# Erf of three batches as a tanh with a polynomial on GpSimd, and later statistics, in a four-layer cross-attention kernel

## What is computed

```python
# layer 2: 16 heads of 16
attn = softmax(Q @ K.T / sqrt(16));  ctx = attn @ V
out = q + gelu(ctx @ Wo + bo, approximate=False)      # x * (1 + erf(x / sqrt 2)) / 2, added to the row

# layer 3: 8 heads of 32
x = residual + mha(layernorm(x), layernorm(ctx))
xn = layernorm(x);  U = (xn @ W_in.T + b_in) @ Bmat
s = silu(s @ A.T) + u_t                                # 512 steps, one after the other
x = x + states @ Cmat + mean(probs) @ W_prog.T + b_prog
```

## Time and profile before

| what | value |
|---|---|
| median of 3 runs | 1514.4 us |
| the profiled execution, its own time | 1517.49 us |
| its span in the trace | 1515.9 us |
| PE, DVE, ACT, POOL busy | 1346.9, 1039.8, 1065.2, 82.9 us |
| mean granted clock of PE | 0.961 |
| scores of the first quad of turns 0 to 3 start at | 341.44, 586.93, 860.87, 1139.6 us |

### The profile page before, as it was taken

The page is one execution under the profiler, slowest core; times in us unless marked ns, Lnnn a source line. Parts: engine busy times, 40 slices in busy tenths (PEclk is TensorE's granted clock), DMA queues, the critical chain, the costliest instruction groups (busy, mean ns, idle before and its releaser), DMA issues.

```text
span 1515.9 us, 35932 instructions
## 1 busy us (share of the span) xinstructions
PE 1346.9 (89%) x13436; PEld 1002.6 (66%) x13436; DVE 1039.8 (69%) x2323; ACT 1065.2 (70%) x3212; POOL 82.9 (5%) x145
## 2 busy tenths in 40 slices
PE   7999899988998889999888999988899999788855
PEld 6788666665675556777666677766676777566644
DVE  4676757756787778687777777877776787777400
ACT  4556677757788887777787677777866777787422
POOL 2000111110000000000000000000000000000000
PEclk9999999999999999999999999999999999999855
DMA  8222310012221122121101211201121121110100
GB/s 296 85 87 98 103 56 2 1 46 95 58 85 42 44 75 68 42 71 57 57 30 57 83 31 58 85 29 54 47 70 43 43 85 57 29 50 9 43 0 14
DMA packets 69883, 90.42 MB, mean 60 GB/s; under 512 B 5520, under 2 KB 58896, under 8 KB 69328
## 3 DMA queue, kind: packets, MB, share of 16 engines
q1 hardware_dynamic: 69600, 87.87, 18.2%
q0 software_dynamic: 112, 0.26, 0.1%
HBM read 71.33 MB, written 16.78 MB: 58 GB/s over the span
## 4 chain that ended last, share of the span: by engine, by line
PE 60%; DVE 14%; ACT 14%; issue 10%; POOL 0%; DMA 0%; ACTq 0%; DVEq 0%; SPq 0%; POOLq 0%
PE ps L1320 14%; PE ps L1694 11%; PE ps L1327 8%; PE ps L1334 7%; PE ps L1723 6%; ACT arena L790 5%; DVE arena L1269 5%; PE ps L1768 3%; PE ps L1397 2%; PE ps L1521 2%; PE ps L1538 2%; PE ps L1677 2%; DVE arena L949 2%; ACT R L850 1%; DVE nmax L1252 1%
## 5 line engine op out<-in xcount | busy, mean ns | idle before, releaser
L1320 PE MATMUL ps<-W,arena 128*128 128x128 f32 x2896 | 434.6, 284 | 22.3 <-ACT arena L790 19.8
L1320 PEld LDWEIGHTS ps<-W,arena 128*128 128x128 f32 x2896 | 324.9, 145 | 171.5 <-issue 129.5
L790 ACT ACTIVATE arena<-ps,nmax 128x512 f32<-128x512 f32 x640 | 435.1, 686 | 0.2
L797 ACT COPY arena<-ps 128x512 f32<-128x512 f32 x320 | 187.3, 585 | 213.0 <-PE ps L1320 208.9
L1249 DVE TENSOR_REDUCE nmax<-ps 128x1 f32<-128x512 f32 x320 | 206.1, 686 | 119.5 <-PE ps L1694 83.3
L1269 DVE COPY arena<-ps 128x512 f32<-128x512 f32 x320 | 213.8, 686 | 23.7 <-PE ps L1320 13.5
L1694 PE MATMUL ps<-W,arena 32*128 32x512 f32 x1280 | 185.2, 646 | 35.3 <-DVE arena L1269 34.2
L1723 PE MATMUL ps<-arena 128*32 128x128 f32 x5120 | 173.4, 276 | 31.6 <-ACT arena L797 31.4
L1252 DVE TENSOR_REDUCE nmax<-ps 128x2 f32<-128x1024 f32 x160 | 193.7, 1210 | 0.0
L1723 PEld LDWEIGHTS ps<-arena 128*32 128x32 f32 x5120 | 130.4, 110 | 69.5 <-ACT arena L797 59.1
L790 ACT ACTIVATION_READ_ACCUMULATOR arena<-ps,nmax 128x1 f32 x640 | 131.1, 205 | 0.0
(11 more groups left out here) (240 smaller groups left out, 1648.0 us busy)
## 6 DMA issues: line engine op xcount, KB each, us to landing
W<-keys SPq DMA_DIRECT2D x48, 512.0 KB, 3.7
arena<-values SPq DMA_DIRECT2D x48, 512.0 KB, 5.1
keys<-W SPq DMA_DIRECT2D x16, 448.0 KB, 3.0
values<-W SPq DMA_DIRECT2D x16, 448.0 KB, 3.6
W<-keys SPq DMA_DIRECT2D x16, 256.0 KB, 2.8
arena<-values SPq DMA_DIRECT2D x16, 256.0 KB, 3.3
W<-in_pack SPq DMA_DIRECT2D x1, 3180.0 KB, 10.5
CX<-in_ctx SPq DMA_DIRECT2D x4, 512.0 KB, 11.0
```

The lines of the kernel that those rows point to most:

```text
L790: nc.scalar.activation(Pr[:, a, :], ps[:, a, :], ACT.Exp, bias=nmax[:, u % 32:u % 32 + 1], accum_out=den[:, u % 32:u % 32 + 1]).then_inc(s ...
L797: nc.scalar.copy(PT[:, (4 * Q + a) % 8, :, :].rearrange("p k n -> p (k n)"), psT).then_inc(sem("u_ev_act"), 1)
L1320: ins = nc.tensor.transpose(dst[:, k * P:(k + 1) * P], src[:, k * P:(k + 1) * P], ident)
```

## The change

Layer 2's exact GELU of batches 0 to 2 is computed as x * (1 + tanh(p(x))) / 2. POOL evaluates the odd polynomial p with 14 instructions on 128x256 tiles (a clamp, a square, a Horner chain of degree 6 in the square, a product), each waiting for the one before, at the chain's step `add`. ACT applies Tanh where it applied Gelu, at step 8 in place of 4. DVE combines with two instructions (`scalar_tensor_tensor`) in place of one sum. Batch 3 keeps Gelu at step 4. The steps behind move: batches 0 to 2 have the row at 9, statistics at 10, nrm and tp at 11, so xT and q at 12 and qT at 13; batch 3 has the row at 5, statistics at 6, nrm and tp at 7, xT and q at 8, qT at 9. Layer 3's statistics go from step 3 to 4, where nrm stays. New buffers `bent` lie in weights that are no longer read.

```diff
 def after_steps(li, b):
-                 2: dict(gelu=4, stats=5, nrm=6, tp=6), 3: dict(bias=2, stats=3, nrm=4, tp=4)}[li])
+                 2: dict(gelu=8, row=9, stats=10, nrm=11, tp=11) if b < 3 else dict(gelu=4, row=5, stats=6, nrm=7, tp=7), 3: dict(bias=2, stats=4, nrm=4, tp=4)}[li])
...
+            def bend(c, b):
+                x, x2, r = bent[b % 2]
+                n = 3 * c + b
+                done = itertools.count(ERF_OPS * n + 1)
+                if n:
+                    pool.wait_ge(sem("L2_gelu"), c * NB + b + 1 - 1)
+                pool.wait_ge(sem("L2_pre"), c * NB + b + 1)
+                nc.gpsimd.tensor_scalar(x, orows[b % 2], ERF_AT, -ERF_AT, ALU.min, ALU.max).then_inc(sem("L2_bent"), 1)
+                pool.wait_ge(sem("L2_bent"), next(done))
+                nc.gpsimd.tensor_tensor(x2, x, x, ALU.mult).then_inc(sem("L2_bent"), 1)
+                pool.wait_ge(sem("L2_bent"), next(done))
+                nc.gpsimd.tensor_scalar(r, x2, ERF_TANH[-1], ERF_TANH[-2], ALU.mult, ALU.add).then_inc(sem("L2_bent"), 1)
+                for a in ERF_TANH[-3::-1]:
+                    pool.wait_ge(sem("L2_bent"), next(done))
+                    nc.gpsimd.tensor_tensor(r, r, x2, ALU.mult).then_inc(sem("L2_bent"), 1)
+                    pool.wait_ge(sem("L2_bent"), next(done))
+                    nc.gpsimd.tensor_scalar(r, r, a, None, ALU.add).then_inc(sem("L2_bent"), 1)
+                pool.wait_ge(sem("L2_bent"), next(done))
+                nc.gpsimd.tensor_tensor(r, r, x, ALU.mult).then_inc(sem("L2_bent"), 1)
...
+                if li == 2 and b < 3:
+                    yield step["add"]
+                    bend(c, b)
...
                 if li == 2:
                     yield step["gelu"]
-                    act.wait_ge(sem("L2_pre"), n)
-                    nc.scalar.activation(nrm[i], orows[i], ACT.Gelu).then_inc(sem("L2_gelu"), 1)
+                    if b < 3:
+                        act.wait_ge(sem("L2_bent"), ERF_OPS * (3 * c + b + 1))
+                        nc.scalar.activation(bent[i][2], bent[i][2], ACT.Tanh).then_inc(sem("L2_gelu"), 1)
+                    else:
+                        act.wait_ge(sem("L2_pre"), n)
+                        nc.scalar.activation(nrm[i], orows[i], ACT.Gelu).then_inc(sem("L2_gelu"), 1)
...
-                    yield step["stats"]
+                    yield step["row"]
                     dve.wait_ge(sem("L2_gelu"), n)
-                    add_more(row, row, nrm[i])
+                    if b < 3:
+                        own["sums"] += 2
+                        nc.vector.scalar_tensor_tensor(orows[i], bent[i][2], 1.0, orows[i], ALU.add, ALU.mult).then_inc(sem("row_sum"), 1)
+                        dve.wait_ge(sem("row_sum"), own["sums"] - 1)
+                        nc.vector.scalar_tensor_tensor(row, orows[i], 0.5, row, ALU.mult, ALU.add).then_inc(sem("row_sum"), 1)
+                        dve.wait_ge(sem("row_sum"), own["sums"])
+                    else:
+                        add_more(row, row, nrm[i])
```

More of the change, by code:

```diff
@@ L1 @@
 from contextlib import ExitStack
+import itertools
 import numpy as np
@@ L132, with after_steps @@
 CUTS = [0] + [PLAN[name][0] for name in ("wk0", "wv0", "inw", "wq0")] + [NPACK]
-def after_steps(li):
+ERF_AT = 5.7
+ERF_TANH = (0.7978849414816304, 0.03633308446488688, -3.2594837808075025e-05, -5.5306259012116404e-05,
+            3.964757753935919e-06, -1.322645093331823e-07, 1.7562063102252576e-09)
+ERF_OPS = 2 * len(ERF_TANH)
+def after_steps(li, b):
     step = dict(rd=0, rdT=1, on=2, wo=2, add=3)
     step.update({0: dict(tp=3), 1: dict(f_tp=3, f_xT=4, f_h=4, bias=5, f_relu=5, f_o=5, stats=6, nrm=7, tp=7),
-                 2: dict(gelu=4, stats=5, nrm=6, tp=6), 3: dict(bias=2, stats=3, nrm=4, tp=4)}[li])
+                 2: dict(gelu=8, row=9, stats=10, nrm=11, tp=11) if b < 3 else dict(gelu=4, row=5, stats=6, nrm=7, tp=7), 3: dict(bias=2, stats=4, nrm=4, tp=4)}[li])
     tp = step["tp"]
@@ L307, in build @@
         orows = [a3.take(D) for _ in range(2)]
+        spare = Carve(W[:, PLAN["inw"][0]:PLAN["outw"][0]])
+        bent = [[spare.take(D) for _ in range(3)] for _ in range(2)]
         oT = [a3.take(4 * P).rearrange("p (q n) -> p q n", q=4) for _ in range(2)]
@@ L506, in chain_of @@
                     return
-                n, step = turn_side(G), after_steps(li)
+                n, step = turn_side(G), after_steps(li, b)
+                if li == 2 and b < 3:
+                    yield step["add"]
+                    bend(c, b)
                 if li:
@@ L741, in chain_of @@
                 c, li, _ = STAGES[G]
-                l, i, n, step = LAYERS[li], b % 2, turn_side(G), after_steps(li)
+                l, i, n, step = LAYERS[li], b % 2, turn_side(G), after_steps(li, b)
                 if l.quads != 2 * (wq + 1):
```

## The result

The changed kernel takes **1494.82 us** (median of 4 runs, 1493.08 to 1495.92), the kernel before 1514.08 beside it (4 runs, 1512.52 to 1514.62): a ratio of 0.9877, 95% interval 0.9865 to 0.9889. That is 19.3 us less.

What follows compares the result with a forecast made beforehand. No engine is full; they hand work round a loop within each quad. Four turns gave -13 us and the clock -1.5: profiled 1517.5 to 1503.0, median 1500 us; forecast range 1494 to 1504, with rivals 1487 to 1512.

Steps and rivals of the forecast that it cites:

- (a): The three quads (batches 0 to 2) that lose a Gelu: together -5.4 us a turn.
- (b): The three quads behind those that lose a Gelu; they lose nrm, tp, xT and q: -1.9 us a turn.
- (c): The three quads that get Tanh and the row ahead of the copies: +0.8 us each, +2.4 a turn.
- (d): The three quads behind the row quads, which get statistics, nrm and tp: +0.35 us each, +1.05 a turn.
- (e): Batch 3 and the first quads of layer 3, which get moved chain steps: together +1.2 us a turn.
- rival 2: Moved work eats most of the gain, stacked layer 3 quads costing 1 us more each: 1507 to 1511; chance 0.18.
- (f): Layer 3's statistics moved to the even half: nearly a swap, -0.1 us each, -0.3 for three a turn.
- (g): PE's clock: fewer long waits of PE should remove some half-clock stretches; -1.5 us taken.
- (h): POOL's polynomial: 7.4 to 11.2 us, 10 taken, so Tanh is not late, by 2 to 6 us.
- Rival 4: Layer 3's stacked quads become a wait ring, PE waiting for ACT's qT: 1514 to 1522; chance 0.03.
- Turn 0: The turn without recurrence, so with more slack in the row quads: perhaps -4 us.
- rival 1: More shows: row hides, even halves take statistics for nothing, half-clock stretches behind Gelus go; about 1488; chance 0.2.

Runs made afterwards that it cites:

- pad5: The changed kernel with five more squares in each POOL polynomial, which change no value: 1499.25 us, ratio 0.9883 to the kernel before.
- bias_even: row_even with layer 1's bias sum also moved from step 5 to 6, into the even half: 1493.24 us, ratio 0.9855 to the kernel before.
- l3_back: The changed kernel with layer 3's statistics back at step 3, ahead of the copies: 1500.41 us, ratio 0.9909 to the kernel before.
- two_op: The changed kernel with the polynomial's additions given a second operation that changes no value: 1493.81 us, ratio 0.9863 to the kernel before.
- erf_only: The kernel before with the tanh and its polynomial alone, statistics right behind the row, layer 3 as before: 1520.39 us, ratio 1.0026.
- row_even: The changed kernel with the row at step 10 in place of 9, behind the copies: 1490.65 us, ratio 0.9844 to the kernel before.
- pad8: The changed kernel with eight more squares in each POOL polynomial, which change no value: 1530.10 us, ratio 1.0106 to the kernel before.

## Why the prediction was right, and where its steps were off

The forecast was 1500 us, and 1494.8 came, within its range; faster by 19.3 us where 14 to 14.5 were worked out.

- **What bounds the kernel** was read rightly: the loop inside a quad, ending with DVE's copies. pad5, bias_even and the root wait show the reverse side: what does not end last costs nothing.
- **(a), (b)**: -7.7 us a turn against -7.3. The "sets of steps" method held to 0.25 us a quad: 5.86 and 6.32 measured for 5.86 and 6.55 forecast.
- **(c)**: +0.52 a row quad in turns 1 to 3, against +0.8. The row costs 0.87 us and DVE had 0.35 of slack ahead of its copies (0.2 of it had been seen between the two copies).
- **(d)**: 0 to +0.33, against +0.35. **(e)**: +0.9 against +1.2; 3c0, where three chains meet, did grow by 1.7 us, as rival 2 asked (0.76 of it by the statistics, see l3_back), but 3b0 and 3b1 together fell by 0.75.
- **(f) is the step that failed.** "This move is nearly a swap", -0.1 each: measured -1.1 us a turn undisturbed (-1.5 in turns 1 and 2) and -1.6 more at the start of turns 2 and 3. The step took the place of the first exponential for the place of the quad's end. The wait for the root was sized well (0.66 to 0.73 us, forecast 0.75), its effect on the first exponential too (0.44, forecast 0.6), but ACT had a wait of 0.40 further on in the same quad. l3_back puts the move at 5.6 us, where the prediction had 0.3 a turn (1.2 in all).
- **(g)**: -1.5 taken, about -6.7 measured in turns 1 to 3 (7.6 less the 0.9 of quad 3d0). The stretches behind Gelus were seen, those at the turn ends not looked for, though the trace before has them (the window of 861.50 above). The price was about right: 0.45 us at most for each us at half clock, where 1.6 for 3.4 is 0.47 and other stretches cost less. The number of stretches was the error: six before (27 us of half clock in the four turns), one after (3.4 us). Elsewhere it went the other way: +0.4 us in turn 0, +1.4 at the start and +2.4 in the tail. Over the whole execution the clock so gave some 2.5 us, near the forecast, but not for its reason.
- **(h)**: 11.15 us, in the bounds of 7.4 to 11.2 but above the 10 taken, since five additions take 0.850 us, more than the 0.73 given as the upper end for a tensor_scalar. The other two took 0.40. The room of 2 to 6 us ahead of Tanh was 1.6 to 2.6.
- **Rival 4** did not come about: where the bank is asked for, PE waits for ACT's qT once in the trace, 0.12 us in turn 0, against the 1.5 us in each such place that the rival needs.
- **Turn 0** gained 2.0 us, not 4: its quads without recurrence are shorter, and so the row shows more (6.16 us against 5.54 for the plain quad), not less. Its slack was assumed from the missing work, not read.
- **Not forecast at all**: +3.2 us in the tail, of which 0.8 is the wait for nrm (1.81 in place of 1.00) and 2.4 a stretch at half clock of open cause. The step that moved layer 3's statistics looked only at the quads, and behind the last quads nothing hides it.

So (c), (d), (e) and (f) all erred to the same side, which is what rival 1 had said (the even halves take work for nothing, half-clock stretches go); against it stood an error in turn 0, the start and the tail. The sum was right in part by luck. Between the profiled executions 14.5 us were forecast and 21.6 came, and the median of 1494.8 lies 0.8 us inside the range's near end. Without the 4.6 us of start and tail, which the forecast did not have, it would have been about 1490, outside that range and in rival 1's.

## What to carry to other kernels

When work moves within a loop that several engines hand round, its price is read at the member that ends the loop, not at the first one it delays: a later wait of the same queue can take the delay up. Of two changes that each look good, count what both leave standing in one quad: the tanh alone made the kernel slower, because row and statistics then held the copies together for 1.7 us and PE's clock fell behind 5 of 12 such quads. And look for waits of PE at stage and turn ends: 0.76 us less there gave 1.6 us more by the clock.

## What the runs showed of the hardware

- GpSimd's tensor_scalar on 128x256 float32 takes 850 ns with one operation (the second None) and 404 with two, in place in both cases (after and two_op). A tensor_tensor of that size takes 727 ns, and 613 where both inputs are the same tile. The Trainium skill (GPSIMD Engine Reference, 4.1 Engine selection) calls one-input operations roughly line-rate; the 404 fit that, being about the 0.41 us of VectorE's sum of that size, the 850 don't.
- A stretch of 3.4 us in which PE is granted 1.2 GHz costs 1.0 to 1.7 us in this kernel: 1.6 in the quads above (8.44 against 6.81, 8.79 against 7.18), 1.7 in turn 0 of erf_only (8.17 against 6.50), 1.0 in the tail (row_even 112.2 against 111.2).
- 96 more squares on GpSimd (pad8) or 27 us less of its work (two_op) left VectorE's copies at 687 ns and its maxima at 686, the values of after: these instructions, which read PSUM, do not feel GpSimd. A small one that reads and writes SBUF does. The copy of the denominators in the timeline of after, first beside a running polynomial, then without one:

```profile
734.42 0.40 POOL L525 TENSOR_SCALAR W<-W 128x256 f32<-128x256 f32 x1
...
734.54 0.36 DVE L1226 COPY arena<-rden 128x128 f32<-128x128 f32 x1
...
746.45 0.23 DVE L1226 COPY arena<-rden 128x128 f32<-128x128 f32 x1
```

  It takes 0.36 us in place of 0.23 and ends as GpSimd's instruction has ended. The 12 such copies beside a polynomial take 0.23 to 0.44 us, 0.35 on average, the 36 others 0.23. That is 0.12 us, once a batch, in an even half: the prediction allowed up to 0.7 for it and added nothing. It also called this copy the only instruction with SBUF alone beside the polynomial; the reciprocal ahead of it is another (from `den` into `rden`), and takes 0.19 us with or without GpSimd.
